# A decoder layer with routed experts: context, weights and mask laid out transposed by the host, half of the query transposition in the first score bank, and all queues ordered anew

## The reference

```python
x = x + attn(layernorm(x))        # 1 head: (xn @ W_qk) @ xn.T / 16 + alibi, causal softmax, @ (xn @ W_v.T)
x = x + xattn(layernorm(x), ctx)  # 16 heads of 16: q from x, k and v from ctx (16, 256, 256), key mask, wfc
x = x + ffn(layernorm(x))         # 8 experts, top 2 of a softmax gate, silu(g) * u, hidden size 1024
```

## Time and profile before

| | us |
|---|---|
| median of 3 runs (lowest, highest) | 1169.71 (1162.94, 1170.6) |
| the profiled execution | 1169.76 |
| its span | 1168.0 |
| prologue, to the copy of the first maxima | 57.0 |
| iteration 0, iteration 1 | 26.7, 29.6 |
| iterations 2 to 13 | 390.4 |
| iteration 14 and last attention | 48.3 |
| expert slots | 616.0 |

### The profile page before, as it was taken

The page is one execution under the profiler, slowest core; times in us unless marked ns, Lnnn a source line. Parts: engine busy times, 40 slices in busy tenths (PEclk is TensorE's granted clock), DMA queues, the critical chain, the costliest instruction groups (busy, mean ns, idle before and its releaser), DMA issues.

```text
span 1168.0 us, 37008 instructions
## 1 busy us (share of the span) xinstructions
PE 1073.2 (92%) x12828; PEld 909.0 (78%) x12828; DVE 655.6 (56%) x2156; ACT 658.0 (56%) x1446; POOL 524.9 (45%) x565
## 2 busy tenths in 40 slices
PE   5799989898889988877898999999999999999996
PEld 4466666666666766643888999999999999999996
DVE  6667756666677766664455444444444444444442
ACT  7587877777777888755443444443443444343442
POOL 7656667566666666523224232323323232333322
PEclk9999989999999999988999999999999999999998
DMA  7745444444555454128512144249222121228321
GB/s 228 239 158 166 161 143 141 152 137 140 168 172 171 158 162 149 55 79 274 224 41 35 34 142 137 36 124 361 37 35 32 32 35 28 36 36 297 82 35 19
DMA packets 91671, 142.76 MB, mean 122 GB/s; under 512 B 20960, under 2 KB 69536, under 8 KB 88288
## 3 DMA queue, kind: packets, MB, share of 16 engines
q1 hardware_dynamic: 75790, 122.95, 31.7%
q0 software_dynamic: 15808, 19.09, 9.7%
q10 hardware_dynamic: 18, 0.01, 0.0%
HBM read 268.13 MB, written 43.47 MB: 267 GB/s over the span
## 4 chain that ended last, share of the span: by engine, by line
PE 83%; another core or an unknown queue 4%; DVE 4%; ACT 3%; issue 2%; DMA 1%; POOL 1%; SPq 1%; ACTq 0%; DVEq 0%; POOLq 0%
PE front L2174 16%; PE t_ring L2174 16%; PE pv L2192 8%; PE s_ring L2192 8%; PE pv L1948 6%; PE front L1780 5%; PE t_ring L1933 5%; PE s_ring L1915 5%; PE front L1789 3%; PE s_ring L1767 2%; PE tail L1767 2%; PE tail L1789 2%; PE front L1853 1%; PE front L1767 1%
## 5 line engine op out<-in xcount | busy, mean ns | idle before, releaser
L766 POOL DMA_INDIRECT out<-y_sb,place_i x71 | 112.2, 1580 | 322.7 <-DVE y_sb L1676 131.4
L2174 PE MATMUL t_ring<-rows_hi,wgu_sb 128*128 128x128 f16 x2272 | 214.8, 220 | 1.2 <-issue 1.2
L2174 PE MATMUL front<-rows_hi,wgu_sb 128*128 128x128 f16 x2272 | 214.9, 220 | 0.7 <-issue 0.7
L1207 DVE TENSOR_REDUCE nmax<-s_ring 128x2 f32<-128x512 f32 x256 | 170.3, 684 | 79.6 <-PE s_ring L1915 78.3
L2174 PE MATMUL front<-rows_lo,wgu_sb 128*128 128x128 f16 x1136 | 198.7, 220 | 1.0 <-issue 1.0
L2174 PE MATMUL t_ring<-rows_lo,wgu_sb 128*128 128x128 f16 x1136 | 198.6, 220 | 0.5 <-issue 0.5
L2174 PEld LDWEIGHTS front<-rows_hi,wgu_sb 128*128 128x128 f16 x2272 | 181.2, 98 | 4.1 <-issue 2.5
L2174 PEld LDWEIGHTS t_ring<-rows_hi,wgu_sb 128*128 128x128 f16 x2272 | 181.3, 98 | 2.6 <-issue 0.9
L908 ACT ACTIVATE probs_t<-t_ring,mask_bias 128x512 f32<-128x512 f32 x256 | 170.0, 697 | 21.6 <-PE t_ring L1933 9.7
L1070 ACT ACTIVATE silu_g<-t_ring 128x256 f32<-128x256 f32 x142 | 54.6, 385 | 170.4 <-PE t_ring L2174 164.2
L1070 ACT ACTIVATE silu_g<-front 128x256 f32<-128x256 f32 x142 | 54.4, 384 | 169.4 <-PE front L2174 161.3
(11 more groups left out here) (263 smaller groups left out, 2146.0 us busy)
## 6 DMA issues: line engine op xcount, KB each, us to landing
wgu_sb<-gu_split SPq DMA_DIRECT2D x71, 2048.0 KB
wd_sb<-down_split SPq DMA_DIRECT2D x71, 1024.0 KB
w_piece<-in_w_gu SPq DMA_DIRECT2D x32, 512.0 KB, 5.6
gu_split<-w_halves SPq DMA_DIRECT2D x32, 512.0 KB, 3.6
w_piece<-in_w_down SPq DMA_DIRECT2D x16, 512.0 KB, 6.5
down_split<-w_halves SPq DMA_DIRECT2D x16, 512.0 KB, 4.3
x_in<-in_x SPq DMA_DIRECT2D x16, 256.0 KB, 2.7
ctx_in<-in_ctx SPq DMA_DIRECT2D x16, 256.0 KB, 3.0
```

Of the source, the lines that this page charges most:

```text
L766: nc.gpsimd.indirect_dma_start(out=out, out_offset=bass.IndirectOffsetOnAxis(ap=place_i[:, j:j + 1], axis=0), in_=y_sb[:, j], in_offset=No ...
L1207: nc.vector.tensor_reduce(nmax[:, n // HJ, :, n % HJ], s_ring[n % 2][:].rearrange("p (r k) -> p r k", r=2), AX.X, ALU.max, negate=True).th ...
L2174: o = nc.tensor.matmul(gu_ring[f][:, part * SLOT:(part + 1) * SLOT], wgu_sb[j][:, w, at:at + P], r[:, j % 2, c], start=(i == 0), stop=(i = ...
```

## The change

**Layouts.** The host hands over ctx transposed (`ctx_t_in`), the weights transposed (wq and wk also in the order of heads that the kernel wants) and the mask in both layouts. The 20 + 2 transposes of weights and mask on PE are gone, and the strided pieces; DVE's `weight_rest` reads `w_raw` in SBUF instead of a PSUM bank. `f_ctxt` on PE is gone: ACT's `f_ctxt` makes both copies straight from `ctx_in`.

**The bank.** `t_half` of query half 0 goes to `s_ring[0]` and waits for the copy of the maxima (`nmt_sb`) instead of `rank_sb`; `h_scores` 0 of the next batch waits for the first division instead. `tail` is first used by `t_ont`.

**Semaphores.** `stacked` is split into `k_stacked` and `q_stacked`.

**Orders.** Every queue is written anew for iterations 0 to 13 and the prologue. PE at the end of an iteration: `h_scores` 15, `t_rank`, `f_v2` (it now waits for `xn2t_sb`), `f_q`, `h_max`, `f_q_rest`; at the start: `t_half` 0, `t_half` 1, `f_xnt`, `h_scores_t` (0,0) and (0,1), `f_k`, `t_ont`, `h_scores_t` (1,0), `f_q1`, (1,1), `h_values` 0, `t_fc`, `f_q1_rest`, `h_scores` 0 and 1. In the prologue the score blocks of batch 0 are laid between the steps of front 1, batch 0's norm is made on DVE instead of POOL, and weights are loaded and split in the order of their use. Iteration 14 keeps its order, written out as `before_last`. In the last slot DVE makes the previous result one step (f) earlier.

```diff
+            load_x(0, 0)
+            load_weight(WQK, w_qk)
+            load_ctx(0, 0)
+            load_weight(WK, wk)
+            load_weight(WV1, w_v)
+            sp.dma_start(slope_sb[:], slope.rearrange("(a n) -> a n", a=1).to_broadcast([P, 1])
+                         ).then_inc(slope_loaded, 16)
+            load_x(1, 1)
+            load_weight(WQ, wq)
+            load_ctx(1, 1)
+            load_weight(WV2, wv)
             sp.dma_start(mask_u8[:], mask).then_inc(consts_loaded, 16)
-            sp.dma_start(slope_sb[:], slope.rearrange("(a n) -> a n", a=1).to_broadcast([P, 1])
...
-                if c:
-                    store_stream(b - 1)
                 if n:
                     load_pieces(b + 3, h + 1 + p, 1 - p)
                 if c:
+                    store_stream(b - 1)
                     store_normed(b - 1, 1 - p)
                 if f and (not isinstance(b, int) or b + 4 < B):
                     load_next(b + 4, p)
                     store_pieces(b + 2, h + 1, p)
                     stack_rows(b + 2, p)
                     stack_k_hi(b + 2, p)
-                    stack_k_lo(b + 2, p)
                 if s and f:
                     stack_max(b + 1, 1 - p)
                 if f:
+                    stack_k_lo(b + 2, p)
                     stack_q_hi(b + 2, p)
                     stack_q_lo(b + 2, p)
...
                     ctx_rest(b + 2)
-                    split_lo(b + 2, 0)
                 if n:
                     rsqrt_norm1(b + 3)
+                    f_norm1(b + 3, 1 - p)
+                if f:
+                    split_lo(b + 2, 0)
                 if c:
                     rsqrt_tail(b - 1)
                 if f:
                     split_lo(b + 2, 1)
-                if n:
-                    f_norm1(b + 3, 1 - p)
-                if f:
                     split_lo(b + 2, 2)
...
+            def weight_hi(i):
+                act.wait_ge(raw_loaded[i], 16)
+                nc.scalar.activation(w_split[:, i, HI], w_raw[:, i], ACT.Copy, scale=PSCALE).then_inc(w_hi, 1)
...
+            def f_ctxt(n, p, u):
+                act.wait_ge(ctx_loaded[p], 16 * u + 16)
+                if not isinstance(n, int) or n > 0:
+                    act.wait_ge(v2_ps, n)
+                nc.scalar.activation(ctx_t[:], ctx_in[:, p], ACT.Copy, scale=XSCALE)
+                nc.scalar.activation(ctx_h[:, HI], ctx_in[:, p], ACT.Copy, scale=XSCALE).then_inc(ctxt_sb, 1)
...
                     h_exp(b, 7, 0)
+                    h_exp(b, 7, 1)
                 if f:
                     f_xn2t(b + 2)
                 if t:
-                    h_exp(b, 7, 1)
-                if f:
-                    f_q(b + 2)
-                if t:
                     h_out(b, p, 3)
                 if s:
                     h_max(b + 1)
                 if f:
                     f_v2(b + 2, p)
+                    f_q(b + 2, 1 - p, h + p + 1)
...
+                if c:
+                    t_recip(b - 1, 0, s_ring[0])
+                    t_recip(b - 1, 1, s_ring[1])
+                    t_divide(b - 1, 0, s_ring[0])
+                    t_divide(b - 1, 1, s_ring[1])
                 if n:
                     f_stats1(b + 3, 1 - p, h + 1 + p)
-                if c:
-                    t_recip(b - 1, 0, tail)
-                    t_recip(b - 1, 1, s_ring[1])
-                if n:
                     f_aggr1(b + 3)
-                if c:
-                    t_divide(b - 1, 0, tail)
-                    t_divide(b - 1, 1, s_ring[1])
...
+                    h_max(b + 1, 14, 15)
                 if c:
                     t_rank(b - 1)
+                if s:
+                    h_max(b + 1, 15, 16)
+                if c:
                     t_pick(b - 1)
                     t_gates(b - 1, 1 - p)
                     t_rows(b - 1, 1 - p)
                     t_pos(b - 1)
+                    t_next_row(b - 1)
                     t_pos_i(b - 1, 1 - p)
-                    t_next_row(b - 1)
-                if s:
-                    h_max(b + 1, 14, 16)
                 if f:
                     f_q(b + 2)
...
+                nc.vector.scalar_tensor_tensor(w_split[:, i, LO], w_raw[:, i], PSCALE, w_split[:, i, HI],
+                                               ALU.mult, ALU.subtract).then_inc(w_lo, 1)
...
-                    if f == 2 and j % 2 == 0 and not first:
+                    last = isinstance(s, int) and s == NSLOT - 1
+                    if f == (1 if last else 2) and j % 2 == 0 and not first:
...
+                elif not isinstance(n, int) or n > 1:
+                    pe.wait_ge(xn2t_sb, n + 1)
...
-                        pe.wait_ge(stacked[p], 16 * STACK_DMAS * (u + 1))
+                        pe.wait_ge(k_stacked[p], 16 * K_STACKS * (u + 1))
+                        pe.wait_ge(q_stacked[p], 16 * Q_STACKS * (u + 1))
                     if n >= 2:
                         pe.wait_ge(smax, 16 * s + n - 1)
-                    elif n == 0 and (later or s > 0):
+                    elif n == 0 and (later or 1 < s < B - 1):
+                        pe.wait_ge(on_sb, 2 * s - 3)
+                    elif n == 0 and s > 0:
...
                 pe.wait_ge(o_sb, 4 * c + 4)
-                if not isinstance(c, int) or c > 0:
+                if not isinstance(c, int) or c < B - 3:
+                    if qt == 0:
+                        pe.wait_ge(nmt_sb, c + 2)
+                elif c > 0:
                     pe.wait_ge(rank_sb, c)
...
                 if c:
-                    t_half(b - 1, q, 0, tail)
-                if f:
-                    f_ctxt(b + 2, p, h + 1)
-                if c:
+                    t_half(b - 1, q, 0, s_ring[0])
                     t_half(b - 1, q, 1, s_ring[1])
                 if f:
                     f_xnt(b + 2)
-                    f_k(b + 2)
                 if t:
```

586 lines of the change are left out of this document (325 added, 261 removed).

## The result

The changed kernel takes 1177.41 us (median of 20 runs, 1169.81 to 1186.89), the kernel before 1170.97 us (20 runs beside it, 1162.9 to 1177.88). The ratio is 1.0056, with a 95% interval of 1.0031 to 1.0082. The profiled execution took 1176.22 us, its span 1174.5.

The account below looks back on a forecast made before the run. PE, busy 92% of the span, was taken to bound the kernel, so only its idle time or work taken off it counts. 1169.8 - 6.5 - 1.4 - 13 - 0.9 = 1148, stated as 1147; range 1116 to 1164, forecast's own 1135 to 1158.

Parts of the forecast that it names:

- Term 1: Prologue: first projections end 8 to 9 us sooner, part of it given back; -6.5 us, between -4 and -9.
- Term 2: Context transposes leave PE, 0.44 us in each of 14 iterations; iterations 0 and 1 together -1.4 us, between 0 and -2.5.
- Term 3: Turn, iterations 2 to 13: new order loses less to late results, 31.4 us each; -13 us, between 0 and -47.
- the hold: Turn: while four scatters run, PE's results reach others late, R + 4.3 to R + 8.8 (R: time of t_rank).
- Term 4: Middle of the iterations: PE has no gap, ACT sets no pace, q stacks stay hidden; nothing at 31.4 us.
- Term 5: Two SBUF operands of weight_rest could delay POOL's rests, at most 1 to 2 us once; left out of the sum.
- Term 6: Last slot: previous result made one step earlier, so the last scatter starts sooner; -0.9 us.
- A: Rival, turn: the hold no longer bites, 29.3 us per iteration, whole 1123 us, span 1112 to 1135; chance 0.27.
- B: Rival, loop: gain given back by middle stalls or the hold's full price; 1160 us, span 1158 to 1181; chance 0.19.
- C: Rival, turn: the hold catches the transposed maxima, 34.8 us per iteration, whole 1189 us, slower; chance 0.09.

Follow-up runs that it names:

- e1: Changed kernel with PE's wait for the gate's weights moved behind its first fronts; 1176.93 us, ratio 1.0036 to the kernel before.
- e2: Changed kernel without its scatters of the entries; 1109.63 us in a single run, iterations 2 to 13 take 339.3 us.
- e8: Changed kernel with filler matmuls in the turn, the gate wait moved and f_q(0) ahead of f_k(1) in the prologue; 1157.3 us, ratio 0.9907.
- e9: Changed kernel with its four scatters apart, one at the turn and three in the middle of the next iteration; 1134.53 us, ratio 0.9703.
- e10: e5 with the transposition of query half 0 put back into tail; 1159.22 us, ratio 0.9925 to the kernel before.
- e15: Changed kernel with four scatters in a row at the turn, each of 32 entries instead of 128; 1180.44 us in a single run.
- e5: Changed kernel with 20 filler matmuls on PE behind t_ont in iterations 1 to 13; 1162.02 us, ratio 0.9951 to the kernel before.
- e4: Changed kernel with all four scatters issued one at a time in the middle of the iteration; 1174.72 us, ratio 1.0016 to the kernel before.
- e14: Kernel before with only its scatters apart, one at the turn and three in the middle of the next iteration; 1135.27 us, ratio 0.9747.
- e7: Changed kernel with only one of the four scatters of a batch; 1114.16 us in a single run.

## Why the prediction was wrong

Two terms failed. The prologue was forecast at -6.5 us and came to +5.3, the turn at -13 and came to +5.2: together 30 us, the distance between 1147 and 1177.

**Term 1, the prologue: -6.5 forecast, +5.3 in the two profiles** (+3.8 between the means of all profiles with the one prologue and the other, 61.5 and 57.7). The step that failed first is "the operands are ready ... the projections end at about 12 to 13". I listed the operands of the first projections and not what PE's queue waits for ahead of them: one line, the wait for the gate's weights, and 5.5 us (PE starts at 7.17 in e1, at 12.62 without it). With the wait moved the projections end at 12.6, as forecast. The second step, "I let 6.5 to 7 us arrive at the first score block", fails even then. The chain of waits of e1:

```profile
11.59 1.76 DVE q_stack L1534
...
22.81 2.56 POOL w_halves L691 x4
25.96 0.74 POOL rstd L615
...
28.20 1.13 PE front L1812 x4
...
35.42 0.60 ACT k_hi L882
36.01 0.50 ACT q_hi L875
...
40.96 0.39 PE s_ring L1950 x2
```

The rstd comes 5.5 us sooner than in the earlier trace rows, the first score block only 2.5 us sooner than the 43.41 of the earlier trace rows: 3 us are lost as front 1's k stands between, on PE and ahead of q on ACT. The 16 score blocks then take 14.9 us to the transposed maxima, instead of 13.2, with front 1's steps between them; I had written "up to 2 us of loss" and taken none. That makes 56.1 against 57.0, and over several profiles nothing at all (57.6 against 57.7). My bounds of -4 to -9 hold neither with the wait nor without it.

**Term 2, iterations 0 and 1: -1.4 forecast, -0.2 in this profile, inside the bounds.** Iteration 1 takes 28.7 instead of 29.6 us. Iteration 0 took 27.4 in this profile with a clock of 0.94, and 25.7 in e2, e8, e9, e10 and e15, where the clock was 1.00; that would make -1.9.

**Term 3, the turn: -13 forecast, +5.** The mechanism was right, and nearly all positions: scatters from R + 2.5, the maxima and the first half ahead of the hold (the second came up to 1.2 us late), xn caught in most turns and let go 1.5 to 2.3 us behind the last scatter's start. The sizes were not: the step that failed is "With 27.8 us of work and 3.6 lost: 31.4 us". The runs make it 28.3 undisturbed (e2), 3.2 for the hold (e5; 3.4 by e8) and 1.5 for the half clock (1.3 by e8), 33.0; for the kernel before 28.4, 3.0 and 1.1, 32.5. So "it costs most of the 2.9 us, and the half clock after it the rest" was too small for the half clock, and the forecast for the changed kernel gave it no price of its own. And what I took for a gain, three of four results ahead of the hold, is none: each order has just one chain through the turn that matters, and here it runs over xn's copy and the first exponential, both caught. `t_fc` starts at R + 12.9, just past my R + 12. PE's stall did not shrink, it moved from before `f_k` to behind `t_ont`. The bound of 0 for this term, on its dear side, did not hold.

**Term 4, the middle: nearly right.** PE waits 0.3 us per iteration there, for the tail's norm, which takes back most of the 0.44.

**Term 5 shows nowhere.** Nothing tells it apart from the spread of the prologue.

**Term 6, the last slot: right.** The last scatter starts 1.29 us behind ACT's `y_sb`, instead of 2.21, 0.9 us sooner; it no longer waits for the one before it:

```profile
1165.60 0.47 ACT L1074 ACTIVATE y_sb<-s_ring,slot_gate 128x256 f32<-128x256 f32 x1 [1.46 <-PE s_ring L2282]
1166.89 1.55 POOL L765 DMA_INDIRECT out<-y_sb,place_i  x1 [4.09 <-ACT y_sb L1074]
```

The rest of the 3.8 us I can only place: behind iteration 14 the kernel before has a stretch with a granted clock of 0.85 (574 to 584 us) that the changed one has not, and no term of the change leads there.

**The rivals.** A did not come, as the hold bites. B comes nearest: the hold at its full price, and the middle taking back what was removed; it had the prologue's gain in it, which there is not. C has the sign, not the cause: the maxima were not caught (copied at R + 2.3). In the Trainium skill's "SBUF — State Buffer", section "Who interferes with whom", a DMA never contends with a compute engine and PE never waits on anyone; these runs differ from it in effect, since 48 scatters of 128 entries of 8 bytes cost 50 to 56 us and PE's results come late. Whether they meet in SBUF, no run shows. Rival A's chance of 0.27, and with it a range that lay low, rested on that section more than the rows allowed.

## What to carry to other kernels

Read a queue from its head: a wait for a constant that stands ahead of the first instruction costs as much as any chain behind it, and the diff shows it in one line. Ask of each stall of PE what it does to the clock afterwards, and price that by itself; the same stall is cheaper if PE runs something in it. Before a slow step is put down to what ran just before it, look for the same step elsewhere in the trace: DVE's slow steps in e4 come without a scatter too. And before reordering work around a disturbance, take the disturbance out once: here that would have shown that the two orders take 28.3 and 28.4 us. The place of four small indirect DMAs was worth 30 us in the kernel before (e14) and 41 us in the changed one (e9, by the ratios 0.9703 and 1.0056), where the new order of everything was worth 1 to 5.

## What the runs showed of the hardware

- Four indirect DMAs issued one behind another on POOL, 1.3 us apart, hold back PE's results: they reach ACT and DVE up to 3.9 us late, in most turns until 1.5 to 2.3 us behind the last one's start. Fewer entries don't shorten it (four of 32 hold as long as four of 128); one alone at the same place delays no result of PE (e7). By what path they do it is open; no run looked for it.
- DVE steps were at times slow beside POOL's split pieces: 1.5 instead of 0.16 us, 1.95 instead of 0.41. That came with a scatter 1.6 us before (e4), and with the last one 13 to 17 us away (the changed kernel, e1, e7).
- Where PE had stood still in the turn, the granted clock was mostly 0.50 for a while behind it; with matmuls in the same gap it stayed at 1.00. It cost the changed kernel 15 to 18 us in 12 iterations, more than any part of the change brought or took. In e1's profile the iterations took back 4.8 of the 6.2 us that the mended prologue had gained, with a clock of 0.94 against 0.95; whether that is more than chance one profile can't say.
- Two profiled executions with the same prologue differ by up to 4.7 us at its end (59.1 to 63.8), so that a single profile can't carry a term of 2 us there.
